# Four cross-attention layers: in the middle two, norm hats, one high part and one relu pair move to the vector engine, and a residual moves by a step

## The reference

```python
sa = _mha(x, x, x, tgt_mask, ...)                     # softmax(q k^T / 4) v, then wo
x = _ln(x + sa, ln1_g, ln1_b)                         # first norm
ca = _mha(x, enc_output, enc_output, memory_mask, ...)
x = _ln(x + ca, ln2_g, ln2_b)                         # second norm
ff = jax.nn.relu(x @ ff_w1 + ff_b1) @ ff_w2 + ff_b2
x = _ln(x + ff, ln3_g, ln3_b)                         # third norm
```

## Time and profile before

| | us |
|---|---|
| median of 3 runs | 3469.91 (3466.33 to 3470.69) |
| profiled execution, its own time | 3477.88 |
| its span | 3476.2 |
| its granted PE clock | 0.957 over the span |

### The profile page before, as it was taken

How to read it: one execution, slowest core, us unless ns; L and a number is a source line. 1 busy time by engine, 2 the same in 40 slices (tenths; PEclk the granted TensorE clock), 3 DMA queues, 4 the chain that set the end, 5 groups by cost and what they waited for, 6 DMA issues and landing times. The chain is left out here.

```text
span 3476.2 us, 81973 instructions
## 1 busy us (share of the span) xinstructions
PE 3076.5 (89%) x28275; PEld 2675.0 (77%) x28400; DVE 1980.9 (57%) x4082; ACT 1959.7 (56%) x7922; POOL 1653.2 (48%) x2002
## 2 busy tenths in 40 slices
PE   7999998699999998458999999998999999848887
PEld 5999997489999998346888888887888888746664
DVE  2455544344444444236777777778777777625665
ACT  2444443234444444236777777777777777626775
POOL 1233323114444454503666666666666666652444
PEclk8999999899999999669999999999999999978998
DMA  2222221311111110312222222233111111122321
GB/s 102 62 72 67 78 72 37 139 34 37 52 51 51 51 44 26 118 51 64 83 71 66 65 70 61 85 102 107 60 49 56 59 59 55 32 76 67 101 86 56
DMA packets 218094, 232.77 MB, mean 67 GB/s; under 512 B 41920, under 2 KB 183232, under 8 KB 215360
## 3 DMA queue, kind: packets, MB, share of 16 engines
q1 hardware_dynamic: 217920, 230.49, 21.0%
HBM read 148.57 MB, written 65.01 MB: 61 GB/s over the span
## 5 line engine op out<-in xcount | busy, mean ns | idle before, releaser
L1735 ACT ACTIVATE middle_stage<-middle_psum,middle_neg_max 128x128 f32<-128x128 f32 x2048 | 727.7, 387 | 358.0 <-DVE middle_neg_max L1715 357.6
L1735 ACT ACTIVATION_READ_ACCUMULATOR middle_stage<-middle_psum,middle_neg_max 128x1 f32 x2048 | 462.6, 226 | 0.0
L1715 DVE TENSOR_REDUCE middle_neg_max<-middle_psum 128x4 f32<-128x512 f32 x512 | 336.8, 679 | 61.8 <-PE middle_psum L1678 61.7
L1689 PE MATMUL middle_psum<-middle_eye,middle_stage 128*128 128x128 f32 x2048 | 320.9, 280 | 19.3 <-DVE middle_p_turned_odd L1721 9.4
L1689 PEld LDWEIGHTS middle_psum<-middle_eye,middle_stage 128*128 128x128 f32 x2048 | 231.8, 142 | 70.8 <-issue 46.2
L1637 POOL COPY middle_inverse_row<-middle_inverse 128x128 f32<-128x128 f32 x256 | 68.5, 297 | 380.0 <-DVE middle_inverse L1604 345.8
L1802 POOL TENSOR_SCALAR middle_n_z<-middle_n_z,middle_n_moments,middle_n_rstd 128x256 f32<-128x256 f32 x192 | 234.7, 1229 | 20.3 <-POOL middle_n_rstd L1797 20.3
L536 POOL TENSOR_TENSOR cross_ff_hidden_lo<-cross_ff_relu,cross_ff_hidden_hi 128x256 fp32r<-128x256 f32 x128 | 101.2, 792 | 278.6 <-DVE cross_ff_hidden_hi L531 278.6
L1917 POOL TENSOR_TENSOR middle_ff_hidden_lo<-middle_ff_relu,middle_ff_hidden_hi 128x256 fp32r<-128x256 f32 x256 | 184.1, 740 | 56.6 <-DVE middle_ff_hidden_hi L1911 56.6
L97 PE MATMUL middle_psum<-middle_n_yt_hi,middle_w_lo 128*128 128x256 f32 x640 | 195.1, 305 | 14.7 <-DVE middle_n_yt_lo L1849 10.0
L1721 DVE COPY middle_p_turned_odd<-middle_psum 128x512 f32<-128x512 f32 x256 | 174.5, 682 | 34.6 <-PE middle_psum L1689 34.5
(11 more groups left out here) (341 smaller groups left out, 10870.1 us busy)
## 6 DMA issues: line engine op xcount, KB each, us to landing
middle_stage<-middle_a_k SPq DMA_DIRECT2D x1024, 16.0 KB, 1.8
middle_xt_hi<-x_hi SPq DMA_DIRECT2D x32, 256.0 KB, 2.7
middle_xt_lo<-x_lo SPq DMA_DIRECT2D x32, 256.0 KB, 3.0
middle_ct_hi<-context_hi SPq DMA_DIRECT2D x32, 256.0 KB, 2.9
middle_ct_lo<-context_lo SPq DMA_DIRECT2D x32, 256.0 KB, 3.1
middle_x_rows<-x_rows SPq DMA_DIRECT2D x32, 256.0 KB, 2.7
middle_mask_flags<-flags SPq DMA_DIRECT2D x128, 64.0 KB, 1.9
x_rows<-middle_n_z SPq DMA_DIRECT2D x32, 256.0 KB, 2.2
```

The lines of the kernel that those rows point to most:

```text
L1689: ins = pe.transpose(banks.psum[:, TURN_BANK, x * SEQ:(x + 1) * SEQ], self.sh.p_wide[:, 4 * b + t, x, :], self.sh.eye[:])
L1715: dve.tensor_reduce(self.sh.neg_max[:, 4 * b + t, :], psum[:, SCORE_BANKS[t], :].rearrange("p (x k) -> p x k", x=4), AX_X, ALU.max, negate ...
L1735: ins = act.activation(self.sh.p_wide[:, 4 * b + t, x, :], psum[:, SCORE_BANKS[t], x * SEQ:(x + 1) * SEQ], ACT.Exp, bias=self.sh.neg_max[: ...
```

## The change

Seven edits, all in the middle layers:

1. `pool_hat` is split for the first and the second norm: POOL keeps variance and reciprocal root (`pool_rstd`), DVE does the two hats (`dve_hat`), placed after the first copy of turned exps of the step. The third norm keeps `pool_hat`.
2. In steps 2 and 4 DVE copies the second turned exps before the third maximum instead of after it.
3. The first norm's high part goes from ACT (`act_hi`) to DVE (`dve_hi`, in front of the low part).
4. The feed-forward's third pair (`m` = 4, step 4) is evicted by DVE (`dve_relu`, behind the first norm's low part), no longer by ACT.
5. POOL's residual leaves step 2 and stands at the end of step 4, for the round after (`Back(r, -1)`).
6. POOL makes the residual of round 0 ahead of the rounds.
7. POOL's wait for the new bias row moves with the residual.

```diff
+    def pool_rstd(self, pool, r):
+        pool.wait_ge(self.moments_ready.sem, self.moments_ready.at(r, B2))
+        pool.sem_inc(self.gate.sem, 1)
+        pool.tensor_scalar(self.variance[:], self.moments[:, :, 1], EPS, None, ALU.add) \
+            .then_inc(self.var_made.sem, 1)
+        pool.wait_ge(self.var_made.sem, self.var_made.at(r, 1))
+        pool.tensor_tensor(self.rstd[:], self.variance[:], self.sh.minus_half[:, 0:B2], ALU.pow) \
+            .then_inc(self.rstd_made.sem, 1)
+    def dve_hat(self, dve, r):
+        dve.wait_ge(self.rstd_made.sem, self.rstd_made.at(r, 1))
+        dve.sem_inc(self.gate.sem, 1)
+        for b in range(B2):
+            dve.tensor_scalar(self.z[:, b, :], self.z[:, b, :], self.moments[:, b, 0:1],
+                              self.rstd[:, b:b + 1], ALU.subtract, ALU.mult) \
+               .then_inc(self.hat_ready.sem, 1)
+    def dve_hi(self, dve, r):
+        dve.wait_ge(self.turned_ready.sem, self.turned_ready.at(r, 1))
+        dve.tensor_copy(self.yt.hi[:], self.y[:]).then_inc(self.hi_ready.sem, 1)
+    def dve_relu(self, dve, r, psum, m):
+        dve.wait_ge(self.hidden_in_psum.sem, self.hidden_in_psum.at(r, m // 2 + 1))
+        for i in range(2):
+            dve.tensor_scalar(self.relu[:, (m + i) % FF_SLOTS16, :], psum[:, EV_BANK, i * T2:(i + 1) * T2],
+                              self.b1[self.stream.of(r)][:, m + i:m + i + 1], 0.0, ALU.add, ALU.max) \
+               .then_inc(self.hidden_ready.sem, 1)
...
@@ ACT, step 4
                     norm1.act(act, r, psum)
-                    norm1.act_hi(act, r)
                 exp(y1_next, 2)
-                if ok(-2):
-                    ff.act_relu(act, Back(r, 2), psum, 4)
                 exp(y1_next, 3)
@@ DVE, step 2 (step 4 alike, with y1 and norm1.dve_hat(dve, r))
                 maximum(x1[2], 0)
                 turned(x1[1], 0)
+                if ok(-2):
+                    norm2.dve_hat(dve, Back(r, 2))
                 maximum(x1[2], 1)
+                turned(x1[1], 1)
                 maximum(x1[2], 2)
-                turned(x1[1], 1)
                 maximum(x1[2], 3)
@@ DVE, step 4
                 turned(y1[1], 2)
                 if ok(0):
+                    norm1.dve_hi(dve, r)
                     norm1.dve_lo(dve, r)
+                if ok(-2):
+                    ff.dve_relu(dve, Back(r, 2), psum, 4)
                 turned(y1[1], 3)
@@ POOL, step 2
                 if ok(-2):
-                    norm2.pool_hat(pool, Back(r, 2))
+                    norm2.pool_rstd(pool, Back(r, 2))
                 lo(x1[0])
-                if stream.is_next(r):
-                    layer.rows_swapped(pool, "o1")
-                if ok(0):
-                    layer.pool_residual(pool, r, norm1.sum_ready)
@@ POOL, step 4
                 if ok(0):
-                    norm1.pool_hat(pool, r)
+                    norm1.pool_rstd(pool, r)
                 lo(y1[0])
+                if stream.is_next(Back(r, -1)):
+                    layer.rows_swapped(pool, "o1")
+                if ok(1):
+                    layer.pool_residual(pool, Back(r, -1), norm1.sum_ready)
@@ POOL, ahead of the rounds
+            layer.pool_residual(pool, 0, norm1.sum_ready)
             run(pool, body)
```

More of the change, by code:

```diff
@@ L2642, in body @@
                 turned(y1[1], 0)
+                if ok(0):
+                    norm1.dve_hat(dve, r)
                 maximum(y1[2], 1)
+                turned(y1[1], 1)
                 maximum(y1[2], 2)
-                turned(y1[1], 1)
                 maximum(y1[2], 3)
```

## The result

The changed kernel takes 3437.84 us (median of 4, 3435.49 to 3439.65) beside 3470.30 of the kernel before: a ratio of 0.9901, 95% interval [0.9883, 0.9919]. It is 32 us faster where 20 were forecast. The profiled executions differ by 38.8 (spans 3476.2 and 3437.4), since that of before lies 8 above its median.

The account below looks back on a forecast made before the run. PE was taken to bound the middle layers, so only its waits could be won. Savings of 0.42 in step 2 and 0.14 in step 4 over 29 rounds, plus 4 us at emptying, gave 3450 us, range 3420 to 3482.

Parts of the forecast that it names:

- Step 2, the hats: Second norm's hats on DVE, 0.66 a pair, end PE's 0.68 wait; ACT's second exps not delayed, hidden by 0.1 only.
- Step 2, what PE keeps: End of step 2: PE is 1.02 ahead, 0.6 becomes a wait for ACT's last exp; saves 0.42 a round.
- Step 4, until the relu: First norm: ACT's eviction moves 0.16 earlier, so PE gains 0.16 of its 0.68 before the third norm's transposes.
- Step 4, the port: DVE's low part stands behind POOL's residual; PE waits 0.75 for DVE's relus; step 4 saves 0.14.
- Rival B: No collision in step 4: step 4 saves 0.9, the round 1.34, giving 3427 us; chance 0.17.
- Rival C: DVE's relus cost the wide row's 0.75 each: step 4 0.56 longer, no change overall, 3470 us; chance 0.22.
- rival D: Slower: DVE's hat pair, from about 0.8, holds up ACT's exps in both steps; at 1.6, 3498 us; chance 0.16.
- The ends: Emptying pipeline, where nothing hides a hat: two waits shrink 1.9 each; with the first norm's last, about 4 us.
- The sum: 0.56 a round over 29 full rounds is 16 us, plus 4 at emptying: 20 off, giving 3450 us.
- The wide range: 3420 to 3482 us, holding the forecast, Rival B and Rival C with some 8 us spread; rival D lies outside.

## Why the prediction was right, and what was mis-sized

- **The bound and the method** held. PE stayed the busy engine, and each step's end was where the forecast put it: ACT's exps in step 2, DVE's relus in step 4.
- **Step 2, the hats.** DVE's pair takes 0.73 from its start to its last end, and the next maximum starts 0.65 behind its start (1884.84 less 1884.19), so that the forecast's 0.66 was right; it starts 0.15 after POOL's root ends (forecast 0.05). The exps behind were hardly held: the second group began 0.01 to 0.03 later in the step than before (in step 2, 1885.56 less 1880.83 is 4.73, before 4.70). The 0.1 of cover was just enough.
- **Step 2, what PE keeps:** forecast 0.42, measured 0.55. The mechanism is the one named, a wait for ACT's last exps, only 0.30 long instead of 0.6. The term mis-sized is ACT's gain. I took the marked idle of 0.27 as all that the eviction could move forward; it moved by 0.41 against the start of the step (1887.19 less 1880.83 is 6.36, before 6.77). An instruction of ACT that waits for nothing starts 0.25 after the start of a 0.4 copy; I had left it 0.43 behind. The 0.31 wait of PE for the copy of turned exps I had not seen; it is hidden before the end. Together: the exps 0.41 earlier and the 0.15 by which they had been ahead of PE give 0.56, measured 0.55.
- **Step 4, until the relu:** PE's early arrival turned into a wait of 0.56 for the norm's eviction. That wait was named, at 0.5. The eviction moved by 0.32 (6.41 into the step, before 6.73) where I took 0.16, the same mis-sizing as in step 2; here the wait for the relus took it up.
- **Step 4, the port:** forecast 0.14, measured 0.40. The collision is right, its length is off: I set the low part's end at 10.44 into the step, it came at 10.13 (1913.86 less 1903.73). I had added the high part's 0.3, the residual's 1.29 and the low part's 0.69 end to end, 2.28 from the end of POOL's attended low part; it took 1.98. By the rows, the residual is 0.18 longer behind the high part (1.47 against 1.29), and the low part ended 0.54 after it. The like holds in every pair of the traces looked at: the second instruction loses what it overlaps with the first, less about 0.14. The low part lost 0.73 of 0.87 in the earlier trace rows, 0.97 of 1.12 in the changed kernel, 1.08 of 1.23 with the hats alone; the residual lost 0.18 of the 0.31 it ran beside the high part. Two such steps are the 0.3 that the sum had too much. The low part's 1.66, forecast at about 1.4, is long only because it starts sooner. The relu pair, 0.86 long and 0.79 to the next instruction's start (1914.57 less 1913.78), was priced right at 0.8.
- **Rival B** (no collision) is refuted for this kernel by the 1.66, and what it would have been worth was found by moving the residual: its 0.9 in step 4 came out as 1.19 (12.08 to 10.89). **Rival C** is refuted by the relu pair's 0.86. The slower **rival D** is refuted by the hats' 0.73, where it begins at about 0.8. The estimate that the prediction set beside it, from the Trainium skill ("VectorE: DVE Perf Modes", "The perf-mode tier table"), a hat at no more than a cast's 0.31, is not borne out: a hat takes 0.41 by mean. There page and measurement differ, and the measurement decides.
- **The rule of the Trainium skill** ("SBUF — State Buffer", "SBUF: two separate sides": whoever starts first holds the shared pair for the whole instruction) agrees with both directions here: with the residual ahead the low part takes 1.66, without it 0.69, and the residual itself takes 1.47 behind DVE's high part, 1.28 to 1.30 where the high part is on ACT or the residual runs elsewhere. The loss, the overlap less about 0.14, is near a full block and not a shared rate. The page has this for a DVE instruction with two inputs in SBUF, which the low part is, or in a mode that uses two ports; that the cast ran in such a mode is shown by no run but for its 0.18 here.
- **The ends.** Forecast 4 us, measured about 6 at emptying (103 to 97) and 6 at filling, of which some 4 are four rounds' ordinary gain. The two hat waits at the end shrank by 1.8 each (4.90 to 3.12, 5.98 to 4.21), forecast 1.9. What of the rest at the two ends belongs to which edit was not resolved: the filling's length varies by some 3 us between kernels whose first rounds should be alike.
- **The sum.** A round gained 0.98 instead of 0.56 by the mean of 25: over 27 rounds 11 us. The ends gained 12 instead of 4. Together 38.8 of span where the forecast had 20. By the medians it is 32; the 6 between are the profiled execution of before, which lies 8 above its median. The wide range holds the result with ease, the forecast's own range (3437 to 3462, 0.1 to 0.9 a round) barely: 3437.8, and 0.98 a round is outside it. That range was itself loosely added: 0.9 in 29 rounds and 4 at the ends come to 3440. No error cancelled another: both steps were priced too low, by 0.13 and 0.26.

## What to carry to other kernels

Trace an ended wait to the end of its step before giving it a price: of the hats' 1.36 a round only 0.33 was left while the next wait in series stood, and two edits worth 0.33 and 0.24 alone were worth 0.85 together. When work goes from an engine to DVE, look what POOL does beside it: a place 3.7 us earlier for one POOL instruction was worth more (0.77 a round) than any single move between engines. Test each part of a bundle alone, and once more with the collision gone: the relu pair's move cost 0.06 a round in one place and brought 0.69 in the other.

## What was not expected of the hardware

- A cast of 512 columns on DVE took 0.43 in the first round of the changed kernel, where no instruction of POOL ran beside it, against 0.69 for the two-input subtraction of the same shape. That is the price forecast (the sum for step 4 used 0.3). In the full rounds it takes 0.58, beginning 0.29 before POOL's attended low part ends. A hat (two operands per partition) is 0.41 by mean, a relu from PSUM 0.47. The two hats of a pair start about 0.32 apart (0.73 less 0.41), two casts of the same width about 0.13 (0.43 less 0.30).

```profile
1546.70 0.43 DVE L1864 CAST middle_n_yt_hi<-middle_n_y 128x512 fp32r<-128x512 f32 x1 [2.63 <-ACT middle_n_y L1852]
```

- ACT starts an instruction that needn't wait 0.25 after the start of a copy that lasts 0.4; with a wait between them, the eviction began 0.70 after it. The mark "idle" showed 0.27 of that.
